# Routing of four sequences shared between VectorE and GpSimd, weight pieces reordered, two early root pairs instead of four

## The reference, cut to what matters

```
x = layernorm(x + self_attention(x))          # learned relative positions
x = layernorm(x + cross_attention(x, ctx))    # causal
logits = x @ router_w.T;  scores = sigmoid(logits);  sfc = scores + bias
# 64 experts in 8 groups of 8: keep the 4 groups with the largest sum of their top two,
# of the experts in these the 8 largest sfc; weights = 2.5 * scores / sum(scores chosen)
y = sum over experts of weight * (relu(x @ up_w)**2 @ down_w) + shared expert
x = layernorm(x + y)
```

## Time and profile before

| | us |
|---|---|
| median of 3 runs | 282.61 |
| lowest, highest | 281.99, 283.95 |
| the profiled execution, its time | 283.57 |
| its span, first to last instruction | 281.8 |
| TensorE busy | 254.9 |
| VectorE busy | 202.9 |
| ScalarE busy | 215.0 |
| GpSimd busy | 140.9 |

### The profile page before, as it was taken

The page is one execution under the profiler, slowest core; times in us unless marked ns, Lnnn a source line. Parts: engine busy times, 40 slices in busy tenths (PEclk is TensorE's granted clock), DMA queues, the critical chain, the costliest instruction groups (busy, mean ns, idle before and its releaser), DMA issues.

```text
span 281.8 us, 5973 instructions
## 1 busy us (share of the span) xinstructions
PE 254.9 (90%) x1912; PEld 202.6 (72%) x1912; DVE 202.9 (72%) x564; ACT 215.0 (76%) x569; POOL 140.9 (50%) x135
## 2 busy tenths in 40 slices
PE   4989999999999999989895769999998999999980
PEld 3579998788888877767663444768786888788850
DVE  2598736778888889978999964588994547755514
ACT  7462660889999999989997766788887897698850
POOL 5009001500111159656364004388998998699970
PEclk9999999999999999999999988999999999999996
DMA  6709320497633316756560002976571895597101
GB/s 125 175 9 398 125 76 0 114 238 263 182 88 97 87 46 141 170 161 179 168 179 1 1 2 86 229 183 187 169 200 31 214 235 172 149 223 196 47 0 37
DMA packets 52243, 37.94 MB, mean 135 GB/s; under 512 B 15794, under 2 KB 43124, under 8 KB 52212
## 3 DMA queue, kind: packets, MB, share of 16 engines
q1 hardware_dynamic: 52212, 37.57, 49.7%
HBM read 30.48 MB, written 7.08 MB: 133 GB/s over the span
## 4 chain that ended last, share of the span: by engine, by line
PE 55%; DVE 12%; POOL 10%; SPq 7%; issue 6%; DMA 5%; ACT 3%; POOLq 1%; DVEq 0%; ACTq 0%
PE bank L723 19%; PE bank L707 10%; POOL unit_lo L634 8%; PE bank L740 5%; PE bank L758 5%; SPq L456 4%; PE bank L768 3%; PE bank L746 3%; DMA qc_dram<-q_lo 2%; PE bank L656 2%; DVE neg_max L1215 2%; SPq L452 2%; PE bank L663 1%; PE bank L785 1%; DMA x_tok<-in_x 1%
## 5 line engine op out<-in xcount | busy, mean ns | idle before, releaser
L634 POOL TENSOR_TENSOR unit_lo<-unit,unit_hi 128x512 fp32r<-128x512 f32 x68 | 86.8, 1299 | 33.5 <-ACT unit_hi L1071 32.2
L979 ACT ACTIVATE probs<-bank,neg_max 128x128 f32<-128x128 f32 x224 | 64.8, 408 | 4.7 <-DVE neg_max L1215 4.5
L1346 DVE SCALAR_TENSOR_TENSOR scaled<-bank,roots 128x512 f32<-128x512 f32 x64 | 43.8, 687 | 28.4 <-PE bank L723 22.4
L1070 ACT ACTIVATE unit<-scaled 128x512 f32<-128x512 f32 x68 | 42.9, 630 | 18.1 <-DVE scaled L1346 17.3
L1215 DVE TENSOR_REDUCE neg_max<-bank 128x4 f32<-128x512 f32 x56 | 38.4, 687 | 11.3 <-PE bank L746 10.7
L1071 ACT ACTIVATE unit_hi<-scaled 128x512 fp32r<-128x512 f32 x68 | 41.9, 617 | 0.0
L758 PE MATMUL bank<-ident,probs 128*128 128x128 f32 x256 | 38.9, 274 | 2.9 <-ACT probs L979 2.9
L758 PEld LDWEIGHTS bank<-ident,probs 128*128 128x128 f32 x256 | 30.2, 140 | 8.0 <-ACT probs L979 5.2
L746 PE MATMUL bank<-k_bd,q_stk 128*128 128x512 f32 x64 | 34.0, 532 | 0.0
L707 PE MATMUL bank<-spread,rel_t 128*128 128x128 f32 x256 | 28.9, 275 | 0.0
L707 PEld LDWEIGHTS bank<-spread,rel_t 128*128 128x128 f32 x256 | 28.7, 192 | 0.1
(11 more groups left out here) (202 smaller groups left out, 478.9 us busy)
## 6 DMA issues: line engine op xcount, KB each, us to landing
roots<-root_dram SPq DMA_DIRECT2D x60, 256.0 KB, 4.5
q_stk<-q_dram SPq DMA_DIRECT2D x16, 128.0 KB, 3.2
k_bd<-k_dram SPq DMA_DIRECT2D x32, 64.0 KB, 2.3
incoming<-in_L_ffn_up_w SPq DMA_DIRECT2D x4, 512.0 KB, 4.5
q_stk<-qc_dram SPq DMA_DIRECT2D x16, 128.0 KB, 3.1
k_bd<-kc_dram SPq DMA_DIRECT2D x32, 64.0 KB, 2.6
incoming<-in_L_ffn_down_w SPq DMA_DIRECT2D x4, 512.0 KB, 4.2
k_dram<-k_hi SPq DMA_DIRECT2D x2, 512.0 KB, 3.5
```

The source lines that it names most:

```text
L634: nc.gpsimd.tensor_tensor(unit_lo[:, k % R], unit[:, k % 3], unit_hi[:, k % R], ALU.subtract).then_inc(lo_ready, 1)
L979: last = nc.scalar.activation(probs[:, U % 3, h4 * L:(h4 + 1) * L], ps[BS[U % 3]][:, h4 * L:(h4 + 1) * L], ACT.Exp, bias=neg_max[:, U % 4, ...
L1070: nc.scalar.activation(unit[:, k % 3], scaled[:, k % 3], ACT.Square)
L1346: ins = nc.vector.scalar_tensor_tensor(scaled[:, k % 3], h, 0.0, roots[:, n % ROOT_RING, c % ROOTS], ALU.max, ALU.mult)
```

## The change

Three parts:

- Weight pieces: piece 5 is loaded right behind piece 4 in SyncE's block 11, and pieces 6 and 7 one block sooner.
- Routing of batches 0 and 1: GpSimd adds 1 to the exponentials (r_one), adds the bias (biased), masks by group (masked), multiplies score by chosen (weight), scales (comb), and makes the root out of ScalarE's results. Each step is handed over by a semaphore of its own, ten in all. GpSimd does this after its pieces, in program order: the low parts of a batch's two sequences, then the batch's share. The factor 0.5 of the root moves into ScalarE's copy to root_t, and the factor 2.5 onto wrec on VectorE. Batch 0 runs at 1.9 parts a step instead of 1.35.
- EARLY is two instead of four: pairs 2 and 3 get their roots by DMA. On ScalarE weights_out stands before queries_out.

```diff
@@ -49,7 +49,7 @@
...
 ROOT_SETS = NPAIR // ROOTS
-EARLY = 2 * ROOTS
+EARLY = ROOTS
 LD = 4
...
@@ -59,7 +59,7 @@
...
-BATCHES = [(range(0, 2), 1.35), (range(2, 4), 2.7), (range(4, 6), 1.4), (range(6, 8), 1.4)]
+BATCHES = [(range(0, 2), 1.9), (range(2, 4), 2.7), (range(4, 6), 1.4), (range(6, 8), 1.4)]
 ROUTE0 = [NG * (NB + seqs[-1]) + USE + 1 for seqs, _ in BATCHES]
...
@@ -135,6 +135,9 @@
...
     return f * CH + (NSH + m * ROOTS if m else 0)
+
+
+PIECES_AT = {NB + 1: (2,), NB + 2: (3,), NB + 3: (4, 5), NB + 4: (6,), NB + 5: (7,)}
...
@@ -505,8 +518,8 @@
...
                     keep(qc_dram, (1,), q_lo, cols, qc_kept[b % 2])
-                if 2 <= B - 7 < NB:
-                    load_piece(B - 7)
+                for n in PIECES_AT.get(B, ()):
+                    load_piece(n)
             for f in range(2):
...
@@ -618,21 +631,58 @@
...
-            for k in range(-1, 2 * CH):
-                if k in (-1, REST2):
-
-                    for b in range(0 if k < 0 else HB, HB if k < 0 else NB):
-                        cols = slice(b * L, (b + 1) * L)
-                        pool.wait_ge(xt_out, NB + b + 1)
-                        nc.gpsimd.tensor_tensor(x2_lo[:, cols], x2_t[:, cols], x2_hi[:, cols],
-                                                ALU.subtract).then_inc(x2_split, 1)
-                if k >= 0:
-
-                    pool.wait_ge(hi_ready, k + 1)
-                    if k >= R:
-                        pool.wait_ge(down_done, k - R + 1)
-                    nc.gpsimd.tensor_tensor(unit_lo[:, k % R], unit[:, k % 3], unit_hi[:, k % R],
-                                            ALU.subtract).then_inc(lo_ready, 1)
+            def tokens_low(b):
+                cols = slice(b * L, (b + 1) * L)
+                pool.wait_ge(xt_out, NB + b + 1)
+                nc.gpsimd.tensor_tensor(x2_lo[:, cols], x2_t[:, cols], x2_hi[:, cols],
+                                        ALU.subtract).then_inc(x2_split, 1)
+
+            def route_share(q):
+
+                seqs = BATCHES[q][0]
+                size = len(seqs)
+                at = slice(seqs[0], seqs[0] + size)
+                pool.wait_ge(logit_exp, seqs[-1] + 1)
+                pool.wait_ge(ld["corr"], 16)
+                nc.gpsimd.tensor_scalar(r_one[:, at, :], r_exp[:, at, :], 1.0, None, ALU.add).then_inc(one_made, 1)
+                pool.wait_ge(sig_made, q + 1)
+                nc.gpsimd.tensor_tensor(biased[:, at, :], score[:, at, :],
+                                        corr_row[:, :].unsqueeze(1).broadcast_to([128, size, E]), ALU.add)\
+                    .then_inc(biased_made, 1)
+                pool.wait_ge(keep_made, q + 1)
+                pool.wait_ge(biased_made, q + 1)
+                nc.gpsimd.tensor_tensor(masked[:, at, :].rearrange("p n (g e) -> p (n g) e", g=EG),
+                                        biased[:, at, :].rearrange("p n (g e) -> p (n g) e", g=EG),
+                                        gkeep[:, at, :].rearrange("p n g -> p (n g)").unsqueeze(2)
+                                        .broadcast_to([128, size * EG, ES]), ALU.mult).then_inc(masked_made, 1)
+                pool.wait_ge(chosen_made, q + 1)
+                nc.gpsimd.tensor_tensor(weight[:, at, :], score[:, at, :], chosen[:, at, :], ALU.mult)\
+                    .then_inc(weight_made, 1)
+                pool.wait_ge(wrec_made, q + 1)
+                pool.wait_ge(weight_made, q + 1)
+                nc.gpsimd.tensor_tensor(comb[:, at, :], weight[:, at, :],
+                                        wrec[:, at].unsqueeze(2).broadcast_to([128, size, E]), ALU.mult)\
+                    .then_inc(comb_made, 1)
+                base, inverse = first_root_tiles(q)
+                pool.wait_ge(root_newton, q + 1)
+                link(nc.gpsimd.tensor_tensor(root_sum[:, at, :], comb[:, at, :], inverse, ALU.mult))
+                link(nc.gpsimd.tensor_tensor(inverse, root_sum[:, at, :], base, ALU.add))
+                nc.gpsimd.tensor_tensor(root[:, at, :], inverse, chosen[:, at, :], ALU.mult).then_inc(root_made, 1)
+
+            for q in range(2):
+                for b in BATCHES[q][0]:
+                    tokens_low(b)
+                route_share(q)
+
+            for k in range(2 * CH):
+                if k == REST2:
+                    for b in range(HB, NB):
+                        tokens_low(b)
+                pool.wait_ge(hi_ready, k + 1)
+                if k >= R:
+                    pool.wait_ge(down_done, k - R + 1)
+                nc.gpsimd.tensor_tensor(unit_lo[:, k % R], unit[:, k % 3], unit_hi[:, k % R],
+                                        ALU.subtract).then_inc(lo_ready, 1)
...
@@ -817,7 +867,7 @@
...
-                pe.wait_ge(root_ready, 2 * (f + 1))
+                pe.wait_ge((root_made, root_ready)[f], 2)
...
@@ -1033,7 +1083,7 @@
...
                     if b in (HB, HB + 2):
-                        act.wait_ge(exp_read, (b - HB) // 2 + 1)
+                        act.wait_ge(one_made, (b - HB) // 2 + 1)
                     nc.scalar.activation(r_exp[:, b % HB, :], ps[BM][:, 0:E], ACT.Exp, scale=-1.0)\
...
@@ -1042,13 +1092,13 @@
...
                         act.wait_ge(qc_kept[n], 16 * 2 * (NB // 2))
-                nc.scalar.copy(root_t[:, f * HT:(f + 1) * HT], ps[(4, BN)[f]][0:E, :]).then_inc(ct_out, 1)
+                nc.scalar.mul(root_t[:, f * HT:(f + 1) * HT], ps[(4, BN)[f]][0:E, :], (0.5, 1.0)[f]).then_inc(ct_out, 1)
...
                 at = slice(seqs[0] % HB, seqs[0] % HB + len(seqs))
-                act.wait_ge(comb_ready, q + 1)
+                act.wait_ge(comb_made if q < 2 else comb_ready, q % 2 + 1)
                 link(nc.scalar.activation(comb_ln[:, at, :], comb[:, at, :], ACT.Ln, bias=tiny_col[:, :]))
...
@@ -1087,12 +1137,12 @@
...
                     tokens_out(at_step(s, TOKENS))
+                if s - 1 in CT:
+                    weights_out(CT.index(s - 1))
                 if at_step(s, USE) is not None:
...
                     first_roots(ROOTS_AT.index(s))
-                if s - 1 in CT:
-                    weights_out(CT.index(s - 1))
                 if at_step(s, GATHERED) is not None:
...
@@ -1254,19 +1304,25 @@
...
                 one, sig, weighted, kept, total, top, replaced, keep, sums = routing_tiles(q)
-                if part == 0:
+                shared_out = q < 2
+                if part == 0 and not shared_out:
                     dve.wait_ge(logit_exp, seqs[-1] + 1)
-                    dve.wait_ge(ld["corr"], 16)
                     if q == 2:
                         dve.wait_ge(pt_out_a, probs_copied(STAGES - 1)[1])
+                        dve.wait_ge(root_made, 2)
                     if q == 3:
-                        dve.wait_ge(root_ready, q)
+                        dve.wait_ge(root_ready, 1)
                     nc.vector.tensor_scalar(one, r_exp[:, all_n, :], 1.0, None, ALU.add).then_inc(exp_read, 1)
-                if part == 1:
-                    dve.wait_ge(exp_read, q + 1)
+                if part == 1 and shared_out:
+                    dve.wait_ge(one_made, q + 1)
+                    nc.vector.reciprocal(sig, one).then_inc(sig_made, 1)
+                if part == 1 and not shared_out:
+                    dve.wait_ge(exp_read, q - 1)
                     mark(nc.vector.reciprocal(sig, one))
-                if part == 2:
+                if part == 3 and shared_out:
+                    dve.wait_ge(biased_made, q + 1)
+                if part == 2 and not shared_out:
                     mark(nc.vector.tensor_tensor(biased[:, all_n, :], sig,
...
@@ -1289,13 +1345,19 @@
...
                 if part == 9:
-                    link(nc.vector.tensor_tensor(keep, replaced[:, :, 0:EG], gscore[:, all_n, 0:EG], ALU.not_equal))
+                    ins = nc.vector.tensor_tensor(keep, replaced[:, :, 0:EG], gscore[:, all_n, 0:EG], ALU.not_equal)
+                    if shared_out:
+                        ins.then_inc(keep_made, 1)
+                        return
+                    link(ins)
                     mark(nc.vector.tensor_tensor(
...
                 if part == 10:
+                    if shared_out:
+                        dve.wait_ge(masked_made, q + 1)
                     for n in range(first, first + size):
...
@@ -1304,14 +1366,25 @@
...
                     link(last)
-                    mark(nc.vector.tensor_tensor(chosen[:, all_n, :], kept, masked[:, all_n, :], ALU.not_equal))
+                    ins = nc.vector.tensor_tensor(chosen[:, all_n, :], kept, masked[:, all_n, :], ALU.not_equal)
+                    if shared_out:
+                        ins.then_inc(chosen_made, 1)
+                        return
+                    mark(ins)
                 if part == 12:
-                    link(nc.vector.tensor_tensor(weighted, sig, chosen[:, all_n, :], ALU.mult))
+                    if shared_out:
+                        dve.wait_ge(weight_made, q + 1)
+                    else:
```

(17 more changed lines are left out.)

## The result

The changed kernel took 291.17 us, the median of 4 runs (290.24 to 293.71), against 282.30 us for the kernel before beside it. The ratio is 1.0336, with a 95% interval of 1.0281 to 1.0391: slower by 3.4%. The forecast was 289.6 us in a range of 286.0 to 292.8.

A forecast was written before the change was run, and what follows sets the result against it. From 138.9 to 165.4 us VectorE, busy 95%, was taken to set the pace. The terms 9.0 - 4.0 + 3.3 + 0.8 - 2.1 = +7.0 us on the median 282.61 gave 289.6 us, range 286.0 to 292.8.

The forecast's parts named there:

- Term 1: At step 51 VectorE waits for GpSimd's r_one add, queued behind piece 7's conversion: +9.0 us.
- Term 2: Routing work leaving VectorE in batches 0 and 1, plus 0.9 us of L1292's contention with GpSimd's cast: -4.0 us.
- Term 3: Three places where VectorE visibly waits for GpSimd hand-overs: +3.3 us, bounds 0 and 4.5.
- (a): Batch 1's r_one add at step 59 stands behind all of batch 0 on GpSimd; VectorE waits 2.0 us.
- (b): Batch 1, step 62: keep and the expert maxima in one step, VectorE waits 0.65 us for a GpSimd product.
- (c): Batch 1, step 63: chosen and the weight sum in one step, VectorE waits 0.65 us for a GpSimd product.
- rival of free hand-overs: Steps after the stall limited by ScalarE, so VectorE's hand-over waits are hidden: +3.7, 286.3 us; chance 16%.
- Term 4: Tail from batch 1's wrec to the last root grows from 2.4 to 3.2 us: +0.8, bounds 0.3 to 1.5.
- Term 5: Two root spreads of 1.05 us fewer on full TensorE: -2.1 us, bounds -2.6 and 0.
- bound of 0 for a late set: Root set 1 arrives late by DMA for pair 2, so fewer spreads bring nothing: 291.7 us; chance 6%.
- TensorE's clock: Rival: after the 9 us stall TensorE's clock drops, six slow steps cost 3.6 us, 293 us; chance 9%.
- the crowding: Two pieces' effect on gathers 12 and 13 costs nothing beyond the stall; rival: stall 12 us, 292.5, chance 4%.

The follow-up runs named there:

- e2: Changed kernel with the weight pieces loaded in the old order, everything else as changed: 295.97 us, ratio 1.0499.
- e4: Changed kernel with GpSimd doing batch 0's token subtractions, r_one add and bias ahead of piece 7's conversion: 282.59 us, ratio 1.0019.
- e8: Changed kernel with no sharing: all routing on VectorE, batch 0 at 1.35, new piece order and two early pairs kept: 282.73 us, ratio 1.0023.
- e9: Kernel before with the new order of the pieces alone: 283.32 us, ratio 1.0043.
- e5: e4 with VectorE adding r_one itself in both batches, and batch 1's biased ahead of its token subtractions on GpSimd: 281.86 us, ratio 0.9972.
- e7: e4 with batch 1's masked, weight, comb and root back on VectorE, r_one still GpSimd's: 281.55 us, ratio 0.9979.
- e3: Changed kernel with four early root pairs again, everything else as changed: 293.45 us, ratio 1.0407.
- e1: Kernel before with two early root pairs instead of four, nothing else: 281.42 us, ratio 0.9965.
- e10: e8 with the old order of the pieces, so only two early pairs and weights_out ahead: 281.12 us, ratio 0.9956.
- e12: e6 with pieces 4 and 5 loaded singly, 6 and 7 together in block 13, batch 0's biased before piece 6: 280.72 us, ratio 0.9939.
- e6: e5 with batch 1's masked, weight, comb and root back on VectorE, only its biased staying on GpSimd: 280.03 us, ratio 0.9920.
- e11: e6 with the old piece order, batch 0's masked on VectorE, its biased before piece 6, and its rate 1.35: 283.21 us, ratio 1.0039.

## Why the prediction was right

The time was right within 0.6% (289.6 against 291.17), and so was the mechanism: the routing stretch grew by 9.5 us where terms 1 to 4 said 9.1. The closeness of the sum has some luck in it. +7.0 was said; the two profiled executions have 7.1, the medians 8.9, and single runs of one kernel lie 3 us apart. The terms also missed to both sides: the hand-overs cost 0.5 more, TensorE's waits 0.5 that the sum hadn't got, and 0.5 was lost ahead of step 51, while the part behind turn_weights came back 0.9 us better. Term by term:

**Term 1, the stall: right.** The links that set it showed: piece 7 issued at 135.10 (said 135.5), converted at 143.2 (143.3), one_made at 144.5 (144.5), the reciprocal at 144.63 (144.6). e2 moved the piece and the stall moved with it; e4 moved the add ahead of the piece, the wait of 9.17 became 1.98 and the routing stretch 8.8 us shorter. That is shown, not argued. Of the 9.1 us between the two reciprocals (144.63 against 135.56) 0.5 stood ahead of step 51 already, so the stall has 8.6 of the stretch. One link was wrong and cost nothing: piece 6 left at 127.90 and not at 129.2, as piece 4 was issued at 120.12, not 121.56, and converted by 127.9. Piece 7 stands behind gather 13, which this didn't move.

**Term 2, what leaves VectorE: right in sum.** gkeep took 0.18 and 0.14 us where batch 0's had taken 1.01. The other instructions' prices were not measured one by one, but the stretch checks the sum. It grew by 9.5 us; the stall was 8.6 of it, the hand-overs 3.8 and the tail 0.6. VectorE's waits for TensorE (below) were 0.9, but the kernel before had one of 0.35 in the stretch as well, so they add 0.5:

```profile
138.51 0.69 DVE L1215 TENSOR_REDUCE neg_max<-bank 128x4 f32<-128x512 f32 x1 [0.35 <-PE bank L746]
```

That leaves -4.0 for this term, as said. e8 and e9 add that gkeep's 0.9 goes with the order of the pieces, also where nothing stalls and nothing is shared (0.17 us in both).

**Term 3, the hand-overs: right in kind, 0.5 too small.** (a) was 2.53 us (said 2.0). The add took 0.53 us where 0.4 was assumed, and from wrec (comb starts at 157.54) to the end of the add (162.42) it was 4.9 us, said 4.6. (b) and (c) were 0.59 and 0.65 (said 0.65 each). Sum 3.8 against 3.3. From e4, e5 removed (a), and the wait ahead of batch 0's reciprocal with it, and won 2.5 us of the stretch; e7 removed (b), (c) and the tail and won 1.5, or 1.1 without the shorter first wait. The rival of free hand-overs has fallen with these two.

**Term 4, the tail: right.** wrec ended at 173.66, the last root at 176.70: 3.0 us, where before it was 2.4; 0.6 against 0.8.

**Term 5, two spreads: right in kind, its size only roughly known.** The sum had 2.1. e3 measured 2.3 us, e1 and e10 1.0 and 1.2. Behind turn_weights the changed kernel's trace has 3.0 us less than the one before, and 2.8 less than e3's. Pair 2 did not wait for its roots in the changed kernel, but it did in e1, where weights_out stood in its old place, and in e2, e7 and e12, where it stood in the new one. So the set being in time is not something that the reordering secures, and the bound of 0 for a late set was a worry for the changed kernel too.

**TensorE's clock: a rival of 9% that was partly there.** The windows of TensorE after the change:

```profile
134.90:144.60 9.70, 2.85 (x31) 0.81 0.54 151
144.60:150.00 5.40, 3.33 (x14) 0.50 0.27 75
150.00:155.00 5.00, 5.00 (x56) 0.88 0.00 2
163.00:168.00 5.00, 3.41 (x14) 0.69 0.00 2
```

After the stall the granted clock is 0.50 for over 5 us, and falls again after the second wait. The rival's price, six steps at 0.6 us, did not come. VectorE waited for TensorE only 0.72 us at 149.14 and 0.16 at 149.99, then had no such wait up to turn_weights. The rival took TensorE as full. After a stall it starts with nothing queued and VectorE ahead of it sets the pace; at half clock it had 3.33 us of work in 5.40. So at most 0.9 us of that rival is in the result, 0.5 more than the kernel before had of such waits, and the mean clock of 0.969 is its mark. The Trainium skill's TensorE: Matmul & The Clock Gate (HAM oscillation) says that a wait for data can make the next tile of work start at the low clock. By that rule, the trace agrees: 0.50 after the stall, and 0.50 after e5's wait of 2.38 us. After a wait of 2.10 us in e8 the granted clock stayed at 1.00.

**The step that was wrong without costing anything: the crowding.** The prediction says that whatever the two pieces do to gathers 12 and 13 falls inside the stall and costs nothing more. For the changed kernel that is what happened: TensorE waited 1.60 us at 129.09, and step 51 still began within 0.5 us of before. But it holds only under the stall. Without the stall the new order costs 1.2 us (e9) to 1.6 us (e8 against e10), although it also spares VectorE some 1.2 us in r_one and gkeep. I had looked for its effect on the chain of gathers and not on the first gather behind it.

**Where the gain went.** The change frees VectorE of some 4 us and gains some 2 at the spreads. It pays 9 for the order on GpSimd, 3.8 for three hand-overs and 0.6 for the tail. Taking back only the order leaves 282.59, no gain; taking back also the hand-overs that show gives 280.03. e6 was expected at 278. In its trace step 51 is 3.1 us late, behind a late gather and slow TensorE steps. e12's trace has step 51 at 133.69, but its stretch is 2.3 us longer, through instructions of VectorE that GpSimd held. What is open: whether the stores and gathers in SyncE's queue can be ordered so that no gather is late, and whether an order of pieces exists that serves GpSimd, delays no gather and holds up nothing of VectorE. That was not run.

## What to carry to other kernels

Before work is handed to another engine, find what is queued in front of it there and what that waits for: here the add took 0.53 us, and its place behind a weight load cost 9. Share only products whose result is needed a step later; each that is needed at once costs about 0.6 us, twice its 0.29 us on VectorE. A cost that is hidden behind a stall comes back when the stall is taken away, so measure each part alone before calling it free.

## What the runs showed of the hardware

- Some VectorE instructions from SBUF to SBUF were held until GpSimd's running conversion ended. gkeep took 1.01 us before, 1.53 in e12 (it ends at 144.82, the subtraction at 144.79), and 0.14 to 0.18 with GpSimd idle; r_one took 1.05 in e12 (it ends at 135.33, the subtraction at 135.25), 1.08 in e1 and 0.86 in e11, and 0.22 in e5, e6, e8 and e9, where no conversion ran beside it. So the 0.54 of r_one before had a hold in it too. r_one has one tensor in SBUF as input, not two. The prediction had counted two-input instructions alone. The Trainium skill's GPSIMD Engine Reference (8. Key points) names VectorE's two-port modes beside two SBUF inputs as what contends with GpSimd; whether r_one runs in such a mode, no run here shows.
- On GpSimd the add of a constant to 128x128 took 0.53 us, longer than a product of two such tiles (0.40 to 0.46).
- With a second load of 512 KB right behind the first, the DMA share was 0.98 for 4 us where it had been 0.79, and the next gather was there 2.65 to 3.82 us after its last issue in six kernels, against 1.85 to 2.33 in four kernels with one load. In e9 it was 1.91 with two loads.
- TensorE's waits of 2.38 us (e5) and 2.17 us (e6) were followed by 2 us at a granted clock of 0.50, one of 2.10 us (e8) by none, the stall of 9 us by over 5 us of it.
